# One transformer layer on one core: the choice of experts split by token tiles, with buffers of its own, and the gates of two value tiles moved

## What is computed

```
def _gate(x, Wsel):
    s = jax.nn.sigmoid(jnp.einsum('bsd,hed->bhse', x, Wsel))
    _, idx = jax.lax.top_k(s, K)                       # K = 2 of E = 8
    mask = jax.nn.one_hot(idx, E, dtype=s.dtype).sum(-2)
    return s * mask

gv = _gate(x, Wsel_v)
v = jnp.einsum('bsd,bhse,hedp->bhsp', x, gv, Wv)       # values, gated by expert
att = softmax(q k / sqrt(P));  o = att v
go = _gate(x, Wsel_o)
src2 = jnp.einsum('bhsp,bhse,hepd->bsd', o, go, Wo)    # outputs, gated by expert
```

## Time and profile before

| what | value |
|---|---|
| median of three runs | 3388.97 us (3387.23 to 3390.75) |
| profiled execution | 3392.11 us, span 3390.0 us |
| TensorE matmuls busy | 3202.1 us, 94% of the span |
| VectorE busy | 2454.9 us, 72% |
| ScalarE busy | 2006.9 us, 59% |
| GpSimd busy | 1574.4 us, 46% |
| chain that ended last | PE 71%, DVE 19%, issue 6% |
| TensorE's granted clock, mean | 0.992 |
| a multiplying step of the choice, 128 columns (L1257, 128 times) | 0.294 us mean |

### The profile page before, as it was taken

One profiled execution on the slowest core, in us unless ns is written; L12 is line 12 of the kernel. 1 busy time (PEld: TensorE's weight loads), 2 busy tenths in 40 slices (PEclk: granted clock), 3 DMA queues, 4 the chain that ended last, 5 costly groups with the idle time before them and its releaser, 6 DMA issues.

```text
span 3390.0 us, 67613 instructions
## 1 busy us (share of the span) xinstructions
PE 3202.1 (94%) x19648; PEld 2398.4 (71%) x19648; DVE 2454.9 (72%) x4716; ACT 2006.9 (59%) x4637; POOL 1574.4 (46%) x1295
## 2 busy tenths in 40 slices
PE   1699999999999999999999999999999999997997
PEld 1577777777777777777777777777777777775886
DVE  6577777777777777777777777777777777775776
ACT  2456666666666666666666666666666666664443
POOL 4143355445444454335533554435544544445666
PEclk9899999999999999999999999999999999998999
DMA  5233333233333332333332332333323423324122
GB/s 165 68 80 87 86 97 87 66 87 97 89 84 80 90 100 71 85 85 98 84 82 74 101 96 70 87 92 94 84 73 79 110 76 85 87 60 127 63 81 75
DMA packets 116487, 295.26 MB, mean 87 GB/s; under 512 B 33888, under 2 KB 54624, under 8 KB 100064
## 3 DMA queue, kind: packets, MB, share of 16 engines
q1 hardware_dynamic: 116448, 294.78, 33.3%
HBM read 262.74 MB, written 31.98 MB: 87 GB/s over the span
## 4 chain that ended last, share of the span: by engine, by line
PE 71%; DVE 19%; issue 6%; ACT 1%; DMA 1%; POOL 1%; DVEq 0%; SPq 0%; POOLq 0%; ACTq 0%
PE bank L710 24%; PE bank L837 14%; PE bank L755 9%; PE bank L811 7%; PE bank L725 5%; DVE nmax L1208 4%; PE bank L782 2%; DVE vm L1229 2%; PE bank L730 2%; PE bank L823 2%; PE bank L953 2%; DVE vm L1272 2%; DVE uf L1311 2%; PE bank L791 2%; DVE vm L1254 1%
## 5 line engine op out<-in xcount | busy, mean ns | idle before, releaser
L579 POOL TENSOR_TENSOR u_l<-uf,u_h 128x512 fp32r<-128x512 f32 x512 | 688.9, 1356 | 717.5 <-ACT u_h L1101 717.4
L1208 DVE TENSOR_REDUCE nmax<-bank 128x1 f32<-128x512 f32 (+3 forms) x1024 | 552.8, 581 | 375.4 <-PE bank L725 369.5
L710 PE MATMUL bank<-wv_h,xx 128*128 128x512 f32 x2048 | 744.8, 410 | 12.0 <-DVE vm L1229 7.1
L1017 ACT ACTIVATE probs<-bank,nmax 128x512 f32<-128x512 f32 (+3 forms) x1024 | 591.4, 610 | 259.1 <-DVE nmax L1208 259.1
L1101 ACT ACTIVATE u_h<-uf 128x512 fp32r<-128x512 f32 x512 | 323.0, 631 | 657.4 <-DVE uf L1311 498.7
L710 PEld LDWEIGHTS bank<-wv_h,xx 128*128 128x128 f32 x2048 | 386.6, 189 | 193.1 <-issue 69.3
L575 POOL TENSOR_TENSOR v_sb<-v_next,zero_hb 128x512 f32<-128x512 f32 x64 | 74.6, 1166 | 893.8 <-PE bank L811 879.2
L837 PE MATMUL bank<-u_h,wo_h 128*128 128x512 f32 x1024 | 433.4, 423 | 34.3 <-issue 27.5
L755 PE MATMUL bank<-ident_sb,probs 128*128 128x128 f32 x3328 | 451.8, 274 | 2.3 <-ACT pt_e L1037 1.2
L755 PEld LDWEIGHTS bank<-ident_sb,probs 128*128 128x128 f32 x3328 | 387.4, 141 | 69.1 <-issue 13.5
L1311 DVE TENSOR_TENSOR uf<-oo,go 128x512 f32<-128x512 f32 x512 | 426.6, 843 | 10.1 <-POOL u_l L579 7.9
(11 more groups left out here) (167 smaller groups left out, 5595.5 us busy)
## 6 DMA issues: line engine op xcount, KB each, us to landing
go<-go_d SPq DMA_DIRECT2D x256, 512.0 KB, 6.6
xx<-xs_d SPq DMA_DIRECT2D x128, 512.0 KB, 5.0
oo<-scale_d SPq DMA_DIRECT2D x128, 128.0 KB, 2.9
a_d<-a_out SPq DMA_DIRECT2D x128, 128.0 KB, 2.3
pt_c<-in_x SPq DMA_DIRECT2D x16, 512.0 KB, 4.7
...
go_d<-go_turned SPq DMA_DIRECT2D x256, 8.0 KB
```

The source lines that it names most:

```text
L579: nc.gpsimd.tensor_tensor(u_l[:, e % 2], uf[:, e % 2], u_h.bitcast(f32)[:, e % 2], ALU.subtract).then_inc(ul_done, 1)
L710: last = nc.tensor.matmul(out, lhs, rhs, start=n == 1, stop=n == 3 * len(chunks))
L1017: nc.scalar.activation(probs[:, s % 2, j, 0:w], sbank[j][:, 0:w], ACT.Exp, bias=nmax[:, 2 * s + j:2 * s + j + 1], **kw).then_inc(exp_done, 1)
L1208: nc.vector.tensor_reduce(nmax[:, 2 * s + j:2 * s + j + 1], sbank[j][:, 0:w], AX.X, ALU.max, negate=True).then_inc(nmax_ready, 1)
```

## The change

The choice of experts is split: CH has four parts instead of two. CH 0 and CH 1 are the first and second half of the choice for token tiles 0 and 1, CH 2 and CH 3 the same for tiles 2 and 3. Each step works on 64 columns instead of 128, and there are 34 steps instead of 17 ahead of the transpose. EX is split in the same way. The intermediate results have buffers of their own, `odds`, `level`, `one` and `two`, instead of pieces of `vm`; EX no longer waits for the previous pair's values.

The table of VectorE changes: V 0 and V 1 go to slot 1, CH 2 and CH 3 to slots 2 and 3, V 4 from slot 5 to slot 4, V 6 from slot 7 to slot 6, U 2 from slot 2 to slot 1, U 6 from slot 4 to slot 5. ScalarE gets EX 0 between P 1 and P 2 and EX 1 behind P 3. The order on TensorE, GpSimd and SyncE stays, instruction by instruction.

```diff
--- before.py
+++ after.py
@@ -43,7 +43,7 @@
            [("QK", 0), ("J", 5), ("QK", 1)],
            [("V", 5), ("J", 6), ("V", 6)],
            [("V", 7), ("ST", 0), ("ST", 1), ("J", 7)]]
-ACT_FILL = [[("P", 0), ("P", 1), ("P", 2), ("P", 3), ("EX", 0), ("UH", 0), ("AC", 0), ("UH", 1)],
+ACT_FILL = [[("P", 0), ("P", 1), ("EX", 0), ("P", 2), ("P", 3), ("EX", 1), ("UH", 0), ("AC", 0), ("UH", 1)],
             [("VA", 0), ("PA", 0)],
             [("UH", 2), ("UH", 3), ("VN", 0)],
             [("UH", 4), ("UH", 5)],
@@ -51,14 +51,14 @@
             [("QH", 0), ("QH", 1), ("UH", 7)],
             [("SQ", 0), ("SK", 0)],
             [("SO", 0), ("SO", 1)]]
-DVE_FILL = [[("CH", 0), ("ON", 0), ("U", 0), ("U", 1)],
-            [("CH", 1)],
-            [("U", 2), ("V", 0), ("U", 3)],
-            [("V", 1), ("U", 4), ("V", 2), ("U", 5)],
-            [("V", 3), ("U", 6)],
-            [("V", 4), ("QL", 0), ("QL", 1), ("U", 7)],
-            [("V", 5), ("RECIP", 0)],
-            [("V", 6), ("V", 7), ("YA", 0)]]
+DVE_FILL = [[("CH", 0), ("CH", 1), ("ON", 0), ("U", 0), ("U", 1)],
+            [("V", 0), ("U", 2), ("V", 1)],
+            [("U", 3), ("CH", 2)],
+            [("U", 4), ("V", 2), ("U", 5), ("CH", 3)],
+            [("V", 3), ("V", 4)],
+            [("U", 6), ("QL", 0), ("QL", 1), ("U", 7)],
+            [("V", 5), ("RECIP", 0), ("V", 6)],
+            [("V", 7), ("YA", 0)]]
 POOL_FILL = [[("VC", 0)],
              [("UL", 0), ("UL", 1)],
              [("UL", 2), ("RP", 0), ("UL", 3)],
@@ -204,7 +204,9 @@
         var = sb("var", [NP, TT])
         root = sb("root", [NP, TT])
         rstd = sb("rstd", [NP, TT])
-        best = sb("best", [NP, TT * 4])
+        best = sb("best", [NP, TT // 2 * 4])
+        odds = sb("odds", [NP, TT, NG])
+        level, one, two = (sb(name, [NP, TT // 2, NG]) for name in ("level", "one", "two"))
 
         rest = rot[:, 0].rearrange("q t g c -> q g t c")
 
@@ -219,7 +221,6 @@
         xn = [rows_view(pc8[:, 4 + 2 * i:6 + 2 * i]) for i in range(2)]
         x_high = [(q_h[:], k_h[:]), (u_h[:, 0], u_h[:, 1])]
         x_low = [(q_l[:], k_l[:]), (u_l[:, 0], u_l[:, 1])]
-        level, one, two, odds = (vm[:, i // 2, i % 2 * (S // 2):i % 2 * (S // 2) + TT * NG].rearrange("q (t n) -> q t n", t=TT) for i in range(4))
 
         hidden_f = [pe8[:, i] for i in range(4)]
         hidden_h = [u_h[:, 0], u_h[:, 1], q_h[:], k_h[:]]
@@ -1051,12 +1052,11 @@
                             act.wait_ge(go_ready, n)
                         nc.scalar.activation(raw[:, i, :], o[:, 0:NPROJ], ACT.Copy).then_inc(free, 1)
                     elif name == "EX":
-                        for t in range(TT):
+                        ts = slice(2 * i, 2 * i + 2)
+                        for t in (2 * i, 2 * i + 1):
                             at, prior, _ = w_at(kind, it, ("P", t))
                             act.wait_ge(w_free[at], prior + 1)
-                        if kind != PRO:
-                            act.wait_ge(v_ready, 8 * n)
-                        nc.scalar.activation(odds, raw[:, :, NQK + NA:], ACT.Exp, scale=-1.0).then_inc(odds_ready, 1)
+                        nc.scalar.activation(odds[:, ts], raw[:, ts, NQK + NA:], ACT.Exp, scale=-1.0).then_inc(odds_ready, 1)
                     elif name == "PA":
                         for t in (TT - 2, TT - 1):
                             at, prior, _ = w_at(kind, it, ("P", t))
@@ -1197,7 +1197,7 @@
             for b in range(B):
                 norm_in(b)
 
-            CHOOSE = 17
+            CHOOSE = 2 * 17 - 1
             n_c = 0
 
             def row_max(s, n):
@@ -1230,10 +1230,10 @@
                     dve.wait_ge(free, count)
                     nc.vector.tensor_reduce(v_next[:, t, j, :], m, AX.X, ALU.add).then_inc(v_ready, 1)
 
-                def choose(half):
+                def choose(pair, half):
 
                     nonlocal n_c
-                    n_c = half * CHOOSE // 2
+                    n_c = pair * (CHOOSE // 2) + half * 8
 
                     def step(ins):
 
@@ -1245,44 +1245,46 @@
                     def groups(ap):
                         return ap.rearrange("q t (g e) -> q t g e", e=E)
 
-                    top = best[:].rearrange("q (t g) -> q t g", t=TT)
-                    top_b = top.unsqueeze(3).to_broadcast([NP, TT, 4, E])
-                    rank_b = rank_sb[:, None, None, :].to_broadcast([NP, TT, 4, E])
+                    ts = slice(2 * pair, 2 * pair + 2)
+                    top = best[:].rearrange("q (t g) -> q t g", t=TT // 2)
+                    top_b = top.unsqueeze(3).to_broadcast([NP, TT // 2, 4, E])
+                    rank_b = rank_sb[:, None, None, :].to_broadcast([NP, TT // 2, 4, E])
 
                     def first_best(dst):
-                        step(nc.vector.tensor_reduce(top, groups(level), AX.X, ALU.max))
-                        step(nc.vector.tensor_tensor(groups(dst), groups(level), top_b, ALU.is_equal))
-                        step(nc.vector.tensor_tensor(groups(dst), groups(dst), rank_b, ALU.mult))
-                        step(nc.vector.tensor_reduce(top, groups(dst), AX.X, ALU.max))
-                        step(nc.vector.tensor_tensor(groups(dst), groups(dst), top_b, ALU.is_equal))
+                        step(nc.vector.tensor_reduce(top, groups(level[:]), AX.X, ALU.max))
+                        step(nc.vector.tensor_tensor(groups(dst[:]), groups(level[:]), top_b, ALU.is_equal))
+                        step(nc.vector.tensor_tensor(groups(dst[:]), groups(dst[:]), rank_b, ALU.mult))
+                        step(nc.vector.tensor_reduce(top, groups(dst[:]), AX.X, ALU.max))
+                        step(nc.vector.tensor_tensor(groups(dst[:]), groups(dst[:]), top_b, ALU.is_equal))
 
                     if half == 0:
-                        for t in (TT - 2, TT - 1):
+                        for t in (2 * pair, 2 * pair + 1):
                             at, prior, _ = w_at(kind, it, ("P", t))
                             dve.wait_ge(w_free[at], prior + 1)
-                        step(nc.vector.tensor_scalar(level, raw[:, :, NQK + NA:], SIG_ONE, None, ALU.min))
+                        step(nc.vector.tensor_scalar(level[:], raw[:, ts, NQK + NA:], SIG_ONE, None, ALU.min))
                         first_best(one)
-                        step(nc.vector.scalar_tensor_tensor(level, one, -BIG, level, ALU.mult, ALU.add))
-                        dve.wait_ge(odds_ready, n + 1)
-                        step(nc.vector.tensor_scalar(odds, odds, 1.0, None, ALU.add))
-                        assert n_c == CHOOSE // 2, n_c
+                        step(nc.vector.scalar_tensor_tensor(level[:], one[:], -BIG, level[:], ALU.mult, ALU.add))
+                        dve.wait_ge(odds_ready, 2 * n + pair + 1)
+                        step(nc.vector.tensor_scalar(odds[:, ts], odds[:, ts], 1.0, None, ALU.add))
                         return
                     first_best(two)
-                    step(nc.vector.tensor_tensor(one, one, two, ALU.add))
-                    step(nc.vector.reciprocal(odds, odds))
-                    step(nc.vector.tensor_tensor(gv[:].rearrange("q t j e -> q t (j e)"), odds[:, :, 0:2 * E], one[:, :, 0:2 * E], ALU.mult))
-                    step(nc.vector.tensor_tensor(go_rows[:].rearrange("q (t n) -> q t n", t=TT), odds[:, :, 2 * E:], one[:, :, 2 * E:], ALU.mult))
-                    if kind != PRO:
-                        dve.wait_ge(go_stored, 64 * n)
-                    nc.vector.transpose(go_turned[:], go_rows[:]).then_inc(go_ready, 1)
-                    assert n_c == CHOOSE, n_c
+                    step(nc.vector.tensor_tensor(one[:], one[:], two[:], ALU.add))
+                    step(nc.vector.reciprocal(odds[:, ts], odds[:, ts]))
+                    step(nc.vector.tensor_tensor(gv[:, ts].rearrange("q t j e -> q t (j e)"), odds[:, ts, 0:2 * E], one[:, :, 0:2 * E], ALU.mult))
+                    last = nc.vector.tensor_tensor(go_rows[:].rearrange("q (t n) -> q t n", t=TT)[:, ts], odds[:, ts, 2 * E:], one[:, :, 2 * E:], ALU.mult)
+                    if pair == 1:
+                        step(last)
+                        if kind != PRO:
+                            dve.wait_ge(go_stored, 64 * n)
+                        nc.vector.transpose(go_turned[:], go_rows[:]).then_inc(go_ready, 1)
+                    assert n_c == (CHOOSE // 2, CHOOSE)[pair], n_c
 
                 def do(job):
                     name, i = job
                     if name == "V":
                         v_gate(i)
                     elif name == "CH":
-                        choose(i)
+                        choose(i // 2, i % 2)
                     elif name == "QL":
                         o, free, _ = w_filled(("QK", i))
                         dve.wait_ge(qk_high, 2 * n + i + 1)
```

## The result

The changed kernel takes 3870.97 us (median of four runs, 3866.18 to 3874.9), the kernel before 3389.86 us in the same comparison: a ratio of 1.1415, with a 95% interval from 1.1392 to 1.1437. That is 481 us slower. The forecast was 3745 us in a range of 3550 to 3850, so the direction was right and the size too small by 126 us.

What follows compares the result with a forecast made beforehand. TensorE was taken to set the pace; a chain 4.6 us longer plus 1.2 us of clock in each of 62 pairs gave 360 us on the 3389.0 us median, stated as about 3745 us, range 3550 to 3850.

Steps and rivals of the forecast that it cites:

- What bounds, and the first two tiles: Inner-loop pair: TensorE sets the pace, 45.87 of 46.45 us; CH 0 and CH 1 fill VectorE's 4.37 us gap free.
- V3's wait: TensorE: V3's weight load stands 0.55 us for a gated value tile; earlier gates would remove this.
- the output product at 32.87: TensorE: starts 0.83 us after the matmul before it, losing 0.60 us, a wait that an earlier gate could remove.
- The hold-up by GpSimd: VectorE: CH 2 takes 3.6 us instead of 2.0, CH 3 5.2 instead of 2.85; row maxima 5 start at 35.8.
- one GpSimd instruction per such step: CH 2 and CH 3: bound taken for each locked step's wait, 0.74 us for rope, 1.30 for a low part of u.
- U6 and ScalarE's queue: U6 behind row maxima 6: copy, rounding, turned scores and later exponentials put 3.25 us into the chain from scores 6 to V5.
- The clock: TensorE's granted clock falls after gaps between the second turn of heads and V5: 1.2 us a pair.
- the 1.7 us for a short fall: TensorE's clock: 1.2 us taken as the short fall in two pairs of three; clock range 0 to 1.7 us.
- rival 2: TensorE's clock falls for long: 62 x (4.6 + 3.4) = 496 us, 3885 us; chance 0.07.
- GpSimd keeps its own pace among the small steps: CH 2 and CH 3: timetable runs GpSimd's rope at 0.74 us and low parts of u at 1.30 us.

Runs made afterwards that it cites:

- The two shifts above: Changed kernel with ScalarE's VN copy ahead of the copies of u 2 and u 3: 3792.32 us; changed kernel with U5 ahead of V2 on VectorE: 3790.86 us.

## Why the prediction was too low

- **What bounds, and the first two tiles: right.** CH 0 and CH 1 take 0.23 us a step in VectorE's old gap, and V3's wait is gone: the weight loads of the values wait for gated tiles 39.7 us in 63 waits before, and 7.1 us in 3 in the changed kernel. One reading there was wrong: the output product at 32.87 did not wait for a gate. It needs the low part of u 4, which GpSimd ended at 32.77 (1730.93, 1.84 us long).
- **The hold-up by GpSimd: right in kind, mis-sized.** This is the step that failed: "CH 2's third locked step waits for 25.5, the next for 26.2, the last for 26.9: 3.6 us instead of 2.0." (A locked step is one that GpSimd can hold up.) It was 4.7 us, because the second locked step, not the third, met the low part of u 2, 0.11 us too late, and one GpSimd instruction more had to pass. U5 lost 0.8 us behind the low part of u 4, which I had not counted; CH 3 took 4.8 us against 5.2 expected. Row maxima 4 came 1.2 us late; 1.2 + 0.8 - 0.4 = 1.6 us: in the forecast's times (the scaling of AT starts at 1714.39 before and at 1697.36 after, 17.03 apart) row maxima 5 start at 37.42 (1720.39 + 17.03 - 1700) instead of 35.8, and V5 at 47.45 instead of 45.9. The chain is 6.1 us a pass, not 4.6: 93 us of the missing 126. The two shifts above, which undo 0.8 and 1.3 us of it, bear this out. The range went wrong with it: it took "one GpSimd instruction per such step" as an upper bound for steps on a timetable of tenths of a us, and left no room for a race lost.
- **Why the step met it: a premise that the change itself moved.** The forecast has "The low part of u 2 starts 2.06 behind row maxima 3, as now". In the kernel before, the copy of u 2 on ScalarE starts just as U2 ends; with U2 moved to slot 1 the copy no longer waits for it. Before, and then after (there in one row with the copy of u 3):

```profile
1723.32 0.67 DVE L1311 TENSOR_TENSOR uf<-oo,go 128x512 f32<-128x512 f32 x1
1724.03 0.63 ACT L1101 ACTIVATE u_h<-uf 128x512 fp32r<-128x512 f32 x1
```

```profile
1706.23 1.15 ACT L1101 ACTIVATE u_h<-uf 128x512 fp32r<-128x512 f32 x2
```

The copy starts 1.35 us behind row maxima 3 before (1722.68) and 1.18 after (1705.05), the low part 2.06 and 1.89. In the forecast's own times the second locked step was ready at about 24.04 (CH 2 at 23.3 and 0.74 for the steps ahead of it) and the low part at 24.1: it took a race as won by 0.06 us without naming it. This is read from the rows; no run moved U2 alone.

- **U6 and ScalarE's queue: right.** Expected 3.25 us in the chain less 0.24 of slack; put in alone it makes V5 2.8 us later and costs 238 us with its clock, and V5 gains 2.4 us where it is undone.
- **The clock: right, slightly small.** Some 1.9 us in 46 of 62 passes, 1.45 in the mean, against 1.2 (16 us). No run shows the 1.7 us for a short fall, from which the 1.2 is taken, nor the 3.4 us of rival 2: they were my estimates. The runs showed 2.0 us for a fall in a long pass (54.64 against 52.64) and none in the short ones. About 12 us lie outside the 62 passes, and the forecast's sum, 3389.0 + 360, is 3749 and not 3745.
- The parts don't add: undone alone they give back 334 (GpSimd), 230 (U6) and 72 us (clock), 636 of 481, as they lie on one chain with TensorE's own work beside it.
- That GpSimd keeps its own pace among the small steps, as in the forecast's timetable: right, its rope takes 0.76 us among them and 0.74 before. Behind U5, a product of 512 columns, the sum of the rope took 1.19 us (1715.07), and in the kernel before 0.74 (1732.73). So a long VectorE instruction held GpSimd up too, by 0.45 us, and a step of 0.23 us by 0.02.
